# A decoder layer: x loads in front of residual stores, later blanks, and the second batch's records over four turns

## What is computed

```
x = x + attention(layernorm(x))          # 4 differential heads, rotary position, wq wk wv wout 512x512
x = x + cross(layernorm(x), ctx, mask)   # softmax over 128 memory rows per batch
x = x + ffn(layernorm(x))

def ffn(h):                              # h: 4096 tokens x 512
    top 8 of 48 present experts by h @ gate.T, weights = softmax over those 8
    each expert keeps its first 192 tokens in token order (CAP); later ones are dropped
    y = (silu(rows @ g.T) * (rows @ u.T)) @ down.T   per expert, 192 rows each
    sum of weight * y back onto each token
```

## Time and profile before

| | |
|---|---|
| median of 3 runs (lowest, highest) | 1068.07 us (1064.69, 1069.98) |
| profiled execution, its own time | 1064.81 us |
| its span, first to last instruction | 1063.1 us |
| busy share of the span: PE, PEld, DVE, ACT, POOL | 96%, 79%, 79%, 59%, 53% |
| granted TensorE clock, mean | 0.986 |
| transfers of the hardware queue (q1) | 145.13 MB |
| transfers that POOL issues (q0) | 40.20 MB |

### The profile page before, as it was taken

One profiled execution on the slowest core, in us unless ns is written; L12 is line 12 of the kernel. 1 busy time (PEld: TensorE's weight loads), 2 busy tenths in 40 slices (PEclk: granted clock), 3 DMA queues, 4 the chain that ended last, 5 costly groups with the idle time before them and its releaser, 6 DMA issues.

```text
span 1063.1 us, 24370 instructions
## 1 busy us (share of the span) xinstructions
PE 1016.1 (96%) x6564; PEld 835.6 (79%) x6564; DVE 835.3 (79%) x2255; ACT 624.7 (59%) x1751; POOL 560.9 (53%) x565
## 2 busy tenths in 40 slices
PE   5999799999999999999999997899999999999994
PEld 4787687887887887887877875688888888888883
DVE  5777587887887887888888876378888888888883
ACT  4555455555545545545555553177777777777772
POOL 3225466566567666666666666623443434434334
PEclk9999899999999999999999999799999999999998
DMA  7999584453331221211311514168999999999995
GB/s 274 376 306 254 209 292 183 145 213 138 101 116 50 77 72 50 87 61 50 98 50 50 210 40 159 41 207 236 255 261 248 263 251 256 262 241 263 252 224 69
DMA packets 90644, 185.75 MB, mean 175 GB/s; under 512 B 23943, under 2 KB 24071, under 8 KB 89712
## 3 DMA queue, kind: packets, MB, share of 16 engines
q1 hardware_dynamic: 59232, 145.13, 42.6%
q0 software_dynamic: 31376, 40.20, 16.8%
HBM read 116.04 MB, written 122.00 MB: 224 GB/s over the span
## 4 chain that ended last, share of the span: by engine, by line
PE 54%; issue 13%; POOL 13%; DMA 9%; DVE 8%; ACT 1%; SPq 1%; DVEq 1%; POOLq 0%; ACTq 0%
PE ps L1236 15%; PE ps L1392 14%; PE ps L1426 9%; POOL slot_records L594 7%; PE ps L1221 5%; DMA arena<-in_x 4%; PE ps L1408 3%; PE ps L1226 3%; POOL rstd L605 2%; DVE qk_both L1058 2%; DMA arena<-slot_records 2%; DMA layer_out<-qk_both,slot_table 2%; POOL arena L650 1%; PE ps L1334 1%; PE ps L1263 1%
## 5 line engine op out<-in xcount | busy, mean ns | idle before, releaser
L594 POOL DMA_INDIRECT slot_records<-row,slot_idx x240 | 243.3, 1014 | 80.2 <-issue 50.8
L679 POOL DMA_INDIRECT layer_out<-qk_both,slot_table x96 | 145.1, 1511 | 218.2 <-DMA layer_out<-qk_both,slot_table 190.7
L605 POOL TENSOR_TENSOR rstd<-mv,neg_half 128x1 f32<-128x1 f32 x96 | 67.8, 706 | 125.5 <-DVE mv L976 78.6
L1236 PE MATMUL ps<-w_high,xn_high 128*128 128x512 f32 x384 | 114.1, 419 | 0.7 <-ACT xn_high L700 0.7
L735 ACT ACTIVATE arena<-ps,neg_max 128x128 f32<-128x128 f32 x256 | 89.9, 377 | 31.9 <-DVE neg_max L968 31.9
L1236 PE MATMUL ps<-w_high,xn_low 128*128 128x512 f32 x384 | 107.3, 401 | 0.0
L1236 PE MATMUL ps<-w_low,xn_high 128*128 128x512 f32 x384 | 107.2, 401 | 0.0
L700 ACT ACTIVATE xn_t<-ps 128x512 f32<-128x512 f32 x64 | 38.3, 599 | 100.8 <-PE ps L1221 100.7
L1392 PE MATMUL ps<-w_high,w_low 128*128 128x192 f32 x576 | 87.8, 274 | 0.0
L1392 PE MATMUL ps<-w_low,w_high 128*128 128x192 f32 x576 | 87.7, 274 | 0.0
L1392 PE MATMUL ps<-w_high 128*128 128x192 f32 x576 | 86.8, 272 | 0.4 <-DVE w_low L1143 0.4
(11 more groups left out here) (164 smaller groups left out, 2468.5 us busy)
## 6 DMA issues: line engine op xcount, KB each, us to landing
gu_sb<-in_gate_up SPq DMA_DIRECT2D x48, 768.0 KB, 5.4
slot_records<-arena SPq DMA_DIRECT2D x6, 3366.0 KB, 25.1
arena<-slot_records SPq DMA_DIRECT2D x48, 280.5 KB, 4.8
dn_sb<-in_down_proj SPq DMA_DIRECT2D x48, 256.0 KB, 5.4
arena<-in_x SPq DMA_DIRECT2D x32, 256.0 KB, 2.7
x_res<-in_x SPq DMA_DIRECT2D x32, 256.0 KB, 3.0
ctx_t_sb<-in_ctx_t SPq DMA_DIRECT2D x32, 256.0 KB, 3.5
ctx_sb<-in_ctx_rows SPq DMA_DIRECT2D x32, 256.0 KB, 4.0
```

Of the source, the lines that this page charges most:

```text
L594: pool.indirect_dma_start(out=records, out_offset=bass.IndirectOffsetOnAxis(ap=slot_idx_of(s)[:, k:k + 1], axis=0), in_=row_of(s), in_offs ...
L605: pool.tensor_tensor(rstd[:, :], mv[:, 1:2], neg_half[:, 0:1], ALU.pow).then_inc(steps.sem, 1)
L679: pool.indirect_dma_start(out=out, out_offset=bass.IndirectOffsetOnAxis(ap=slot_table[0:PART[h], 2 * d.index + h:2 * d.index + h + 1], axi ...
L1236: last = pe.matmul(dst, left[:, c, :], right[:, m, c, :], start=(n == 0 and c == 0), stop=(n == 2 and c == KC - 1))
```

## The change

Four things are changed. In turns 4, 5 and 6 SP issues the next x tile in front of the residual store (`x_first`). The two high-rank blanks are issued at the end of turns 4 and 5. Batch 1's eight scatters leave turn 6; two of them are issued at the end of each of turns 7 to 10, and they count on a semaphore of their own (`d_second`), so the counts that odd batches wait for are one batch lower. POOL's wait for the high-rank blanks stands at the head of batch 2's scatters in turn 7. As this needs certain batches named in turns 8 to 11, `FIRST` is 6: turns 8 to 11 are written out and the loop has nine passes.

```
-        PAIRS, FIRST, LAST = (NB + 6) // 2, 4, NB // 2 - 1
+        PAIRS, FIRST, LAST = (NB + 6) // 2, 6, NB // 2 - 1
...
                 n, c, r = b["norm"].next(), b["cross"].next(), b["route"]
+                x_first = any(r.is_(k) for k in range(3))
+                if x_first:
+                    load_x(n)
                 if r.exists():
                     sp.wait_ge(out_p.sem, out_p.after(r, "rstd"))
                     sp.dma_start(out[bass.ds(r.index * P, P), :], x2[:, r.parity, :])\
                       .then_inc(d_x2[r.parity], 16)
-                if n.exists() and not b["norm"].first():
+                if n.exists() and not b["norm"].first() and not x_first:
                     load_x(n)
...
-                for g, at in enumerate((3, 4)):
+                for g, at in enumerate((4, 5)):
                     if b["norm"].is_(at):
                         fill_high(g)
...
-            sp.wait_ge(d_slot[1], 16 * 8 * (NB // 2 - 1))
+            sp.wait_ge(d_slot[1], 16 * 8 * (NB // 2 - 2))
+            sp.wait_ge(d_second, 16 * 8)
...
-                filling = s.first() or s.is_(1)
-                early = s.exists() and not filling
+                filling = s.first()
+                early = s.exists() and not filling and not s.is_(1)
                 scale(out_p, out_v, o, rstd3, mv3)
                 if early:
+                    if s.is_(2):
+                        pool.wait_ge(s_empty_high, 16 * HIGH_PIECES)
                     scatter_ready()
                     scatter(0)
...
-                if s.is_(1):
-                    pool.wait_ge(s_empty_high, 16 * HIGH_PIECES)
...
                 if filling:
                     scatter(4, 5, 6, 7)
+                for step in range(4):
+                    if s.is_(2 + step):
+                        for k in range(2 * step, 2 * step + 2):
+                            scatter_of(Batch(0, 1, NB), k, d_second)
...
                     if s.back(2).exists() and not (s.is_(2) or s.is_(3)):
-                        dve.wait_ge(d_slot[s.back(2).parity], moved(s.back(2), 8))
+                        dve.wait_ge(d_slot[s.parity], moved(s.back(2 + 2 * s.parity), 8))
```

More of the change, by code:

```diff
@@ L311, in decoder_layer @@
         d_slot = [sem("slots_scattered0"), sem("slots_scattered1")]
+        d_second = sem("second_batch_scattered")
         d_last = [sem(f"last_batch_scattered{n}") for n in range(8)]
@@ L589, in turn, with scatter_of @@
                 n, p, a, c, o, s = (b[k] for k in ("norm", "project", "attend", "cross", "route", "slots"))
+                def scatter_of(s, k, done):
+                    pool.indirect_dma_start(
+                        out=records,
+                        out_offset=bass.IndirectOffsetOnAxis(ap=slot_idx_of(s)[:, k:k + 1], axis=0),
+                        in_=row_of(s), in_offset=None,
+                        bounds_check=SLOTS - 1, oob_is_err=False).then_inc(done, 16)
                 def scatter(*ks):
                     for k in ks:
[L594 to L599, removed]
+                        scatter_of(s, k, d_last[k] if s.is_(NB - 1) else d_slot[s.parity])
                 def scale(steps, ready, b_, rstd, mv):
@@ L991, in turn @@
                     if r.back(2).exists() and not (r.is_(2) or r.is_(3)):
-                        dve.wait_ge(d_slot[r.back(2).parity], moved(r.back(2), 8))
+                        dve.wait_ge(d_slot[r.parity], moved(r.back(2 + 2 * r.parity), 8))
                     dve.tensor_scalar(row_of(r)[:, 0:DM], x2[:, r.parity, :], mv3[:, 0:1], rstd3[:, :],
```

## The result

The changed kernel takes 1056.67 us (median of 6 runs, 1055.75 to 1058.99), the kernel before 1067.12 (6 runs, 1063.59 to 1069.98): ratio 0.9907, 95% interval 0.9884 to 0.9931, so 10.4 us or 0.9% faster. The forecast was 1056, with a range of its own of 1053 to 1060.

What follows compares the result with a forecast made beforehand. PE's matmuls were taken as the bound, with turns 5 and 6 lengthened by waits for x. The terms 10.24 + 0 + 0 + 0.7 = 10.9 us gave 1053.9 to 1057.2; forecast 1056, range 1053 to 1060.

Steps and rivals of the forecast that it cites:

- What bounds the kernel, and where 10 us lie: First stage: PE's matmuls set a turn's length; turns 5 and 6 hold about 10 us more, from late x tiles.
- Both waits go, 10.24 us: Turns 5 and 6: DVE's waits for x vanish, slow clock included, 2.44 + 7.80 = 10.24 us; lower bound 2.44.
- Landings: x tiles for turns 5 to 7: x(5) lands by about 70 us, x(6) by 92, x(7) a us after 109 to 119.
- The 21.3 us taken for the second blank's run: Second high-rank blank: issued between 86 and 98 us, assumed to take 21.3 us again, so landing at 109 to 119.
- the wait moves with the blanks: Rival, turn 7: x(7) or loads behind the second high blank make DVE wait; gain 3 to 8 us, chance 0.10.
- Batch 1's records, 0 us: Turns 7 to 10: two added scatters, 2.54 us, fit POOL's idle 2.46 to 2.64 us; cost 0, nearby bound 1.2.
- POOL becomes the bound: Rival, turns 7 to 10: slower scatters make POOL late, 4 us in all, 10.2 without any cover; chance 0.06.
- POOL's wait for the high blanks, 0 us: Head of turn 7: POOL arrives at 122.7 us, the blank lands at 109 to 119; cost 0, cover 4 to 13.
- Written out, 0.7 us: Turns 8 to 11 out of the loop: 19.44 instead of 19.61 us a turn, 4 x 0.17 = 0.7 us gained.
- bounds 0 and 0.8: Range given for the gain, in us, from writing turns 8 to 11 out of the loop.
- PE's marks are right and the end is not 10.9 us earlier: Sign of a wrong prediction: a later stage takes the gain back, which nothing in the profile shows.
- The sum: Whole kernel: 10.24 + 0 + 0 + 0.7 = 10.9 us gained; forecast 1056 us, chance 0.80.

Runs made afterwards that it cites:

- The second median: The changed kernel, unaltered, measured again in a later group on one chip, against the kernel before: 1060.87 us, ratio 0.9925.

## Why the prediction was right, and where not

- **What bounds the kernel, and where 10 us lie:** right. Turns 5 and 6 held them, and the waits for x with the slow clock behind them were the cause. The kernels that keep the blanks at `(3, 4)` keep the waits, those with the blanks later lose them.
- **Both waits go, 10.24 us:** 10.08 measured (turns 4 to 7). But the sizes of the waits before vary: the kernel with only FIRST changed issues the same work up to turn 8 and took 85.40 us in turns 4 to 7 where the earlier trace rows give 88.00. The wait is worth 7.5 to 10 us, and the prediction took one profile's value.
- **Which part takes them away:** the prediction gave the later blanks and x first together, and x first no place of its own in the sum. The runs give it zero with the later blanks, and nothing without. Of x(5) the prediction says that it follows the last low blank; that holds only because the high blank was moved out of that place.
- **Landings:** 69.1, 90.1 and 116.8 measured, against "by about 70", "by 92" and 110 to 120. The 21.3 us taken for the second blank's run was 27.1 from issue to landing; since the blank was issued early (88.99, in a bracket of 86 to 98), x(7) kept a cover of 8 us, in 3 to 13. So half of the rival "the wait moves with the blanks" came true: the blank ran longer. Issued at 98 it would by the same 27.1 us have landed at 125, when DVE asks (124.84).
- **Batch 1's records, 0 us:** right, with the cover used to the tenth. The rival "POOL becomes the bound" was real by its mechanism: with six more scatters in one turn it took 8.2 us. The two scatters that were added took 0.98 and 0.97 us, beside a DVE that was busy for 3.97 of the 4 us from 139 to 143. The Trainium skill (SBUF — State Buffer, section "SBUF: two separate sides") gives about 3.1 us for a DMA issued from GpSimd beside a DVE copy that holds the shared ports. The trace does not show such a stall here, and nothing here shows whether one of these DVE operations holds those ports.
- **POOL's wait for the high blanks, 0 us:** right: the second blank landed at 116.1, and POOL's rstd in front of that place only began at 123.41. With the blanks alone, where the wait stayed in turn 6, it cost 4.9 us in that turn.
- **Written out, 0.7 us:** the turns themselves gave 0.64. The step that failed is its bound: "bounds 0 and 0.8" took the turns left in the loop to be untouched, and they got 2.53 us dearer (355.7 to 356.0 in the six profiles with the moved records and FIRST = 6, 353.2 to 353.4 in the three with FIRST = 4), as PE's weight loads wait for DVE in each pass. With FIRST alone the loop got 1.15 dearer, so this edit by itself loses 0.6 us instead of gaining 0.7; with the moved records, for which it was made, the loss is 1.9. The prediction named what it would look like ("PE's marks are right and the end is not 10.9 us earlier") and held that nothing in the profile spoke for it.
- **The sum:** for turns 4 to 11 10.9 us was forecast and 10.72 came. For the whole, the parts that repeat are 10.72 - 2.53 = 8.2 us, and with waits of the smaller size about 6; the two measured differences are 10.4 and 6.5 us. That the median fell within 1 us of the forecast owes something to chance. The second median, 1060.87, lies just outside the forecast's range of 1053 to 1060, and three others of kernels with the same turns 4 to 11 lie beside it (1060.77, 1060.82 and 1060.56; x first makes no difference in them), so 6.5 us is nearer to what the change is worth than 10.4. And the parts did not add up as forecast: in the profiled pair the start (+1.62) and the last stage (-2.03) cancelled, and the loop's loss was not foreseen. The sign, the place and the size in turns 4 to 11 follow from the argument; the last two us do not.

## What to carry to other kernels

A long transfer that nobody waits for yet belongs behind the short ones that are wanted soon, by turns and not by a few places in one queue: moving x in front of a store did nothing while a 3366 KB blank stood in front of both. Moving such a transfer later moves its own reader's wait, so look first who reads it, and give that reader's work the idle time that a row shows, not more (two scatters in 2.6 us were free, eight cost 8.2). When turns are written out of a loop, measure the turns that stay in it too, and look for what they wait for among the weight loads as well as the matmuls.

## What the runs showed of the hardware

- A turn in the loop costs 19.63 us in the kernel before, 19.70 with the same body and four more turns written out in front of it, 19.77 in the changed kernel and 19.45 written out; in one program the sum of 18 turns repeats to 0.05 us. The difference shows as short waits of PE's weight loads, 0.2 to 0.4 us each, that PE's own rows hardly show.
- The first high blank ran at 192 GB/s in the stretch shown (195 in the earlier trace rows), in whichever turn it was issued, and the issue of a 256 KB load behind it took SP up to 10.64 us, in which it issued nothing else.
- The granted clock fell to 0.50 to 0.68 at 24 to 28 us in ten of thirteen profiles, in one program with and without, each time behind a wait of PE of 1.8 us or more where the other three had 1.4 or less; turn 2 got 0.8 to 2.3 us longer. In the ten the clock had risen sooner (third group of matmuls 1.09 to 1.46 us against 1.89 to 1.91), so PE came sooner to the same wait: here a sooner rise made the first turns longer, 60.5 to 62.4 us to the mark of turn 4 against 59.4 to 59.6.
